# Softmax sums inverted once per batch element, and row maxima turned on TensorE and masked into extra query rows

## What is computed

```python
x = x + xattn(layernorm(x), ctx)    # 16 heads of 96, 4 key/value heads
x = x + ffn(layernorm(x))           # 8 experts of 512 x 512, the mean of the top 2
# xattn, per batch element:
hidden = concatenate([context, latents])            # 1556 rows
q = latents @ Wq.T; k = hidden @ Wk.T; v = hidden @ Wv.T
attn = softmax(q @ k / sqrt(96)); out = (attn @ v) @ Wo.T
# ffn: logits = x @ W_gate + b_gate; y = relu(x @ W_e + b_e), averaged over the two best experts
```

## Time and profile before

| | us |
|---|---|
| runs | 3805.85, 3798.13, 3792.36 (median 3798.13) |
| profiled execution | 3799.79 |
| its span | 3798.0 |
| TensorE busy | 3615.9 (95%) |
| VectorE busy | 2438.7 (64%) |
| ScalarE busy | 1740.3 (46%) |
| GpSimd busy | 829.2 (22%) |
| mean granted clock of TensorE | 0.979 |

### The profile page before, as it was taken

The page is one execution under the profiler, slowest core; times in us unless marked ns, Lnnn a source line. Parts: engine busy times, 40 slices in busy tenths (PEclk is TensorE's granted clock), DMA queues, the critical chain, the costliest instruction groups (busy, mean ns, idle before and its releaser), DMA issues. The chain is left out here.

```text
span 3798.0 us, 66233 instructions
## 1 busy us (share of the span) xinstructions
PE 3615.9 (95%) x22164; PEld 3291.2 (87%) x22164; DVE 2438.7 (64%) x3568; ACT 1740.3 (46%) x3236; POOL 829.2 (22%) x440
## 2 busy tenths in 40 slices
PE   8999999999999999999999999999999999888999
PEld 7888888888888888888888888888888889766887
DVE  4356666666666666666666666666666666645544
ACT  3234444554545544555545455445555545423222
POOL 0132222222222222222222222222222221431000
PEclk9999999999999999999999999999999999998999
DMA  6531111111111111111111111111111111474100
GB/s 217 199 98 47 47 47 47 47 47 47 47 47 47 47 47 47 47 47 47 46 42 47 47 47 47 47 47 47 47 47 47 47 47 37 120 213 140 39 33 31
DMA packets 302735, 240.04 MB, mean 63 GB/s; under 512 B 197346, under 2 KB 263138, under 8 KB 302066
## 3 DMA queue, kind: packets, MB, share of 16 engines
q1 hardware_dynamic: 302706, 239.69, 21.8%
HBM read 184.38 MB, written 55.22 MB: 63 GB/s over the span
## 5 line engine op out<-in xcount | busy, mean ns | idle before, releaser
L746 PE MATMUL ps_proj<-wv_hi,parts 128*125 128x384 f32 x3072 | 893.4, 347 | 0.0
L135 POOL TENSOR_SCALAR parts<-raw 128x1000 fp32r<-128x1000 f32 (+1 forms) x198 | 267.1, 1349 | 2480.8 <-PE ps_proj L746 2293.1
L680 DVE TENSOR_TENSOR probs_lo<-probs,probs_hi 125x448 fp32r<-125x448 f32 (+1 forms) x896 | 660.8, 754 | 100.2 <-ACT probs_hi L604 76.0
L733 PE MATMUL ps_proj<-parts,wk_hi 128*128 128x500 f32 x2304 | 710.9, 390 | 4.7 <-DVEq L636 4.7
L746 PEld LDWEIGHTS ps_proj<-wv_hi,parts 128*125 128x125 f32 x3072 | 582.3, 193 | 1.6
L650 DVE TENSOR_TENSOR values_lo<-ps_proj,values_hi 125x384 fp32r<-125x384 f32 x384 | 210.7, 555 | 571.9 <-ACT values_hi L588 570.9
L596 ACT ACTIVATE probs<-ps_scores 125x448 f32<-125x448 f32 (+1 forms) x896 | 462.0, 516 | 168.5 <-PE ps_scores L797 130.9
L746 PE MATMUL ps_proj<-wv_lo,parts 128*125 128x384 f32 x1536 | 531.1, 346 | 0.0
L733 PEld LDWEIGHTS ps_proj<-parts,wk_hi 128*128 128x128 f32 x2304 | 431.7, 188 | 94.3 <-DVEq L636 5.1
L137 POOL TENSOR_TENSOR parts<-raw,parts 128x1000 fp32r<-128x1000 f32 (+1 forms) x198 | 496.1, 2505 | 16.5
L604 ACT CAST probs_hi<-probs 125x448 fp32r<-125x448 f32 (+1 forms) x896 | 484.0, 540 | 28.5
(11 more groups left out here) (149 smaller groups left out, 5983.8 us busy)
## 6 DMA issues: line engine op xcount, KB each, us to landing
raw<-in_ctx SPq DMA_DIRECT2D x192, 500.0 KB, 3.6
qk_hi<-proj_out_hi SPq DMA_DIRECT2D x60, 224.0 KB, 2.0
qk_lo<-proj_out_lo SPq DMA_DIRECT2D x60, 224.0 KB, 2.2
queries_hi<-qk_hi SPq DMA_DIRECT2D x32, 336.0 KB, 3.6
queries_lo<-qk_lo SPq DMA_DIRECT2D x32, 336.0 KB, 3.6
att_t<-attended SPq DMA_DIRECT2D x128, 84.0 KB
raw<-att_t SPq DMA_DIRECT2D x7, 768.0 KB, 6.7
att<-att_t SPq DMA_DIRECT2D x7, 768.0 KB, 7.8
```

Of the source, the lines that this page charges most:

```text
L680: dve.tensor_tensor(prs[1][0:R, u % PRING, 0:N], pr[0:R, u % PRING, 0:N], f(prs[0][0:R, u % PRING, 0:N]), ALU.subtract).then_inc(p_lo, 1)
L733: mm = pe.matmul(pproj[n % 2][:, 0:CS], w["wk"][a][:, j // 3, i * P:(i + 1) * P], ct[v][:, c, j // 3, :], start=(j == 0), stop=(j == 3 * K ...
L746: mm = pe.matmul(pproj[n % 2][0:VT, 0:KD], ct[a][:, t // VTC, j // 3, s], w["wv"][v][:, j // 3, :], start=(j == 0), stop=(j == 3 * KT - 1))
```

## The change

Sums: `store` now copies and stores all 97 rows of a head, so the plain row sums go to a DRAM tensor. In the next batch element, SyncE loads the 16 x 56 sums of the one before, VectorE inverts them in one instruction behind unit 14, and SyncE stores the inverses to DRAM, where `combine` reads them as before. SyncE's store waits for VectorE. The sums of batch element 30 are handled between the loop and the loads of the output weights, those of 31 at the start of `combine`.

Maxima: `mrow` is transposed on TensorE (`turn_max`, behind value tile 5), and VectorE multiplies the first eight rows of the result, repeated eight times, with a mask that keeps each half of a group's queries in its own row (`place_max`). They become rows 96 to 103 of `queries_hi`; rows 96 to 103 of `keys_lo` are -1. The diagonals, the matmuls with ones and ScalarE's copy go. `READY = 6`: the first scores come one value tile later, behind tile 6. The parts are spread as one behind each of the six key tiles of chunks 1 and 2, and two in each of the value tiles 0 to 4.

```diff
...
-READY = 5
+READY = 6
...
+def load_sums(sp, stream, scratch, b):
+    sp.dma_start(stream["sums"][:], scratch["z"].rearrange("h (b q) -> b h q", q=Q)[b]).then_inc(stream["sums_loaded"], 16)
+def invert_sums(dve, stream, b):
+    dve.wait_ge(stream["sums_loaded"], b * 16 + 16)
+    dve.reciprocal(stream["inverse"][:], stream["sums"][:]).then_inc(stream["inverted"], 1)
+def store_inverse(sp, stream, scratch, b):
+    sp.wait_ge(stream["inverted"], b + 1)
+    sp.dma_start(scratch["rz"].rearrange("h (b q) -> b h q", q=Q)[b], stream["inverse"][:]).then_inc(stream["inverse_stored"], 16)
...
-def early_parts(c, i):
-    first = (c - 1) * KV
-    return [(0, 0), (first, first + 1), (first + 1, first + 3), (first + 3, first + 4)][i + 1 if c else 0]
+def key_part(c, i):
+    return (c - 1) * KTILES + i
+def value_parts(t):
+    first = (CHUNKS - 1) * KTILES + 2 * t
+    return first, first + 1
...
 def attend(nc, w, stream, io, scratch):
...
         with nc.Block() as block:
             @block.sync
...
-                def store_sums(b, h):
-                    sp.wait_ge(z_inverted, START + b * H + (h + 1) * G)
-                    sp.dma_start(rz_d[bass.ds(b, 1), h * G:(h + 1) * G, :],
-                                 osb[HD:HD + 1, h % 2, :].rearrange("d (h q) -> d h q", q=Q)).then_inc(stored[h % 2], 16)
                 def store(b, h):
...
-                    if h < KV - 1:
-                        store_sums(b, h)
+                    sp.dma_start(z_d[bass.ds(b, 1), h * G:(h + 1) * G, :],
+                                 osb[HD:HD + 1, h % 2, :].rearrange("d (h q) -> d h q", q=Q)).then_inc(stored[h % 2], 16)
...
-                sp.wait_ge(consts, 5)
+                sp.wait_ge(consts, 3)
                 load_v(0)
-                with sp.Fori(0, B - 1) as b:
+                def batch(b, first=False):
                     for n in range(LOADS):
...
+                    if not first:
+                        for i in range(2):
+                            sp.wait_ge(stored[i], START + b * 64)
+                        load_sums(sp, stream, scratch, b - 1)
+                        store_inverse(sp, stream, scratch, b - 1)
                     for h in range(KV - 1):
...
                     load_v(b + 1)
...
-                    store_sums(b, KV - 1)
+                batch(0, first=True)
+                with sp.Fori(1, B - 1) as b:
+                    batch(b)
+                for i in range(2):
+                    sp.wait_ge(stored[i], START + (B - 1) * 64)
+                load_sums(sp, stream, scratch, B - 2)
+                store_inverse(sp, stream, scratch, B - 2)
                 for n in range(LOADS):
...
                 for h in range(2):
...
                 for i in range(2):
...
+                sp.wait_ge(inverse_stored, (B - 1) * 16)
...
                 for h in range(2, KV):
...
-                store_sums(B - 1, KV - 1)
                 for i in range(2):
...
             @block.gpsimd
             def _(pool):
...
+                for n, ap in enumerate((f(vt_hi[:, NVT]), f(vt_lo[:, NVT]), mrow[:], ident[:], own[:])):
+                    pool.memset(ap, 0.0).then_inc(cleared, 1)
+                    pool.wait_ge(cleared, n + 1)
+                for n, (ap, value) in enumerate(((kt[1][HD:HD + HALVES], -1.0), (vt_hi[:, 0:NVT, :, HD:HD + 1], 1.0),
+                                                 (vt_hi[0:Q, NVT, :, HD:HD + 1], 1.0))):
+                    pool.memset(f(ap), value).then_inc(consts, 1)
...
+                pool.affine_select(out=ident[:], in_=ident[:], compare_op=ALU.not_equal, fill=1.0, base=0,
...
+                pool.wait_ge(consts, 4)
+                pool.affine_select(out=own[:], in_=own[:], compare_op=ALU.not_equal, fill=1.0, base=0,
+                                   pattern=[[-1, HALVES], [0, HALF]], channel_multiplier=1).then_inc(consts, 1)
...
-                    act.copy(osb[0:HD, h % 2, :], pav[0:HD, h % 2, 0:GQ]).then_inc(o_copied, 1)
+                    act.copy(osb[:, h % 2, :], pav[0:HD + 1, h % 2, 0:GQ]).then_inc(o_copied, 1)
...
                 with act.Fori(0, B) as b:
                     for c in range(CHUNKS):
...
                             keys(b, c, i)
                     for t in range(NVT):
                         values(b, t)
-                        if t == READY:
-                            act.wait_ge(mb_done, b + 1)
-                            act.copy(q[0][HD:HD + 1, :], pav[HD:HD + 1, :, 0:KV * HALF]).then_inc(mneg_done, 1)
                         if t >= READY:
...
             @block.vector
             def _(dve):
...
-                    dve.tensor_reduce(mrow[:].unsqueeze(2), mpart[:], AX.X, ALU.max).then_inc(mrow_done, 1)
-                    dve.wait_ge(mrow_done, b + 1)
-                    for i in range(2):
-                        shape = [HALF, KV, HALF]
-                        dve.tensor_tensor(mdiag[:, i, :].rearrange("p (a b) -> p a b", a=KV),
-                                          negident[:].unsqueeze(1).broadcast_to(shape),
-                                          mrow[:, i * KV:(i + 1) * KV].unsqueeze(2).broadcast_to(shape),
-                                          ALU.mult).then_inc(mdiag_done, 1)
+                    dve.tensor_reduce(mrow[:, 0:HALVES].unsqueeze(2), mpart[:], AX.X, ALU.max).then_inc(mrow_done, 1)
+                def place_max(b):
+                    dve.wait_ge(max_turned, b + 1)
+                    shape = [HALVES, HALVES, HALF]
+                    dve.tensor_tensor(q[0][HD:HD + HALVES, :].rearrange("p (a b) -> p a b", a=HALVES),
+                                      pav[0:HALVES, 0, 0:HALF].unsqueeze(1).broadcast_to(shape), own[:],
+                                      ALU.mult).then_inc(max_in_queries, 1)
...
-                def invert_sums(b, h, g):
-                    dve.wait_ge(pv_done, START + b * NU + (h + 1) * UNITS)
-                    dve.wait_ge(stored[h % 2], START + b * 64 + 32 * (h // 2))
-                    s = slice(g * Q, (g + 1) * Q)
-                    dve.reciprocal(osb[HD:HD + 1, h % 2, s], pav[HD:HD + 1, h % 2, s]).then_inc(z_inverted, 1)
                 def batch(b, first=False):
                     for c in range(CHUNKS):
                         for i in range(KTILES):
                             keys(b, c, i)
-                            n = c * KTILES + i
-                            if not first and n < G:
-                                invert_sums(b - 1, KV - 1, n)
-                            for p in range(*early_parts(c, i)):
-                                part_max(b, p)
+                            if c > 0:
+                                part_max(b, key_part(c, i))
                     for t in range(NVT):
-                        p = EARLY_PARTS + 2 * t
+                        p, last = value_parts(t)
                         if p < PARTS:
...
+                        if t == READY - 1:
+                            place_max(b)
                         values(b, t)
                         if p < PARTS:
-                            part_max(b, p + 1)
-                        if p + 2 == PARTS:
+                            part_max(b, last)
+                        if last + 1 == PARTS:
...
                         if t > READY:
...
                     for u in range(NVT - READY - 1, NU):
...
-                        if u > UNITS and 1 <= u % UNITS < 1 + G:
-                            invert_sums(b, u // UNITS - 1, u % UNITS - 1)
+                        if u == 2 * UNITS and not first:
+                            invert_sums(dve, stream, b - 1)
...
-                for g in range(G):
-                    invert_sums(B - 1, KV - 1, g)
...
             @block.tensor
             def _(pe):
...
-                def spread_max(b):
-                    pe.wait_ge(mdiag_done, 2 * b + 2)
+                def turn_max(b):
+                    pe.wait_ge(mrow_done, b + 1)
...
-                    pe.wait_ge(z_inverted, START + b * H)
-                    for i in range(2):
-                        mm = pe.matmul(pav[:, i, 0:KV * HALF], ones[:], mdiag[:, i, :], start=True, stop=True)
-                    mm.then_inc(mb_done, 1)
+                    pe.transpose(pav[:, 0, 0:HALF], mrow[:], ident[:]).then_inc(max_turned, 1)
...
                 def scores(b, u):
...
                         if u == 0 and n == 0:
...
-                            pe.wait_ge(mneg_done, b + 1)
+                            pe.wait_ge(max_in_queries, b + 1)
...
                     if j == 0 and h >= 2:
...
-                        pe.wait_ge(z_inverted, START + b * H + (h - 1) * G)
...
                     for n, t in enumerate(tiles):
...
                     for c in range(CHUNKS):
                         for i in range(KTILES):
...
-                            for p in range(*early_parts(c, i)):
-                                max_scores(b, p)
+                            if c > 0:
+                                max_scores(b, key_part(c, i))
```

(46 more changed lines are left out.)

7 lines of the change are left out of this document (4 added, 3 removed).

## The result

The changed kernel takes 3634.29 us (median of four runs, 3631.96 to 3637.84) against 3801.99 before; the ratio is 0.9562, with a 95% interval of 0.954 to 0.9585. The profiled execution took 3633.99 us, 165.8 less than that of before. The gain was forecast at 135 us, 31 too little.

The account below looks back on a forecast made before the run. The prediction took TensorE, busy 95% of the span, as the bound. Its terms, 91.3 - 8 + 43 + 10 + 18 - 18.6 - 0.6 = 135 us, off the profiled 3799.8 gave 3664.5 us, range 3638 to 3708.

Parts of the forecast that it names:

- the spread maxima: TensorE's waits for the maxima parts in key and value tiles: 10 us gained, bounds -5 and 25.
- the transpose: New 112-column transpose on TensorE behind value tile 5: 0.25 us each, 32 times, costing 8 us.
- the tile gap: TensorE between value tiles 5 and 6: waits and matmuls with ones go, 91.3 us gained.
- the tail: Last batch element: output-weight loads behind the inverses' store start GpSimd 18.6 us later, costing 18.6, bounds 14 and 23.
- the reciprocals' term: TensorE's second wait for the probabilities in each loop element goes, the first stays: 18 us gained, bounds 0 and 35.
- case from below: Both waits for the probabilities gone (17) and the maxima's last waits gone (15 less) would give 3635 us.
- The mask: VectorE's 8 x 896 mask from PSUM takes 1.1 us, hidden behind value tile 6 and two score matmuls.
- The clock: TensorE's clock in the 31 loop elements returns to full: 43 us gained, bounds 0 and 43.
- rival 1: TensorE's clock stays low in the loop behind smaller remaining waits: 3707 us, or 3686 for half; chance 0.13.
- 2 (the slow mask): VectorE's mask takes 3.6 us, TensorE waits 1.7 us an element and the clock falls: 3760 us; chance 0.05.
- 4 (the waits move): Waits at the transpose, in value tile 0 and for the probabilities stay or grow: together 3718 us; chance 0.06.
- Rival 3: SyncE issues head stores late behind unit 14's inverses, stopping ScalarE and TensorE: slower, 3867 us at 6.5 us late; chance 0.03.

Follow-up runs that it names:

- before_ready_6: The kernel before with `READY = 6` and nothing else, diagonals and ones kept behind value tile 5: 3720.7 us, ratio 0.9787.
- spread_undone: The changed kernel with the parts of the maxima placed where they were before: 3643.3 us, ratio 0.9596 to the kernel before.
- maxima_only: The changed kernel with the old sums (512 reciprocals on one partition, stored per head): 3630.8 us, ratio 0.9551 to the kernel before.
- sums_only: The kernel before with the new sums alone, diagonals and ones as they were: 3779.4 us, ratio 0.9955.
- tail_fixed: The changed kernel with the six output-weight loads moved ahead of the store of batch element 30's inverses: 3619.1 us, ratio 0.9536 to the kernel before.

## Why the prediction was right in its direction, and wrong in its size

What bounds the kernel, that the place behind value tile 5 cost waits, matmuls and clock, and that the tail would lose: all held. The size was too small. The step that failed most is the term of the spread maxima, 10 us forecast and 20 measured; the transpose, the tile gap and the tail were each 4 us off in the same direction, and the reciprocals' term rested on a wait that the reciprocals do not cause. The range was too narrow below by the prediction's own numbers: its case from below, 17 and 15 us more than the forecast, gives 3632.5 (it says 3635), and its edge was set at 3638, above it. By its own steps, with the forecast and what was measured:

- **The tile gap, 91.3 forecast.** I took the six score matmuls at 0.13 us, from four that stood behind a refill. At full pace they start 0.108 apart (1430.13 to 1430.78, six of them, 0.65), so 3.0 us an element went, not 2.9: 4 us more.
- **The transpose, 8 us.** 0.12 us of TensorE's time each instead of 0.25, and no wait came before it: 4 us more. Its duration is 259 ns as median of 32 (259 to 287), over half of it beside the matmuls around it, so the cost can't be read off a duration; the prediction's lower bound, 0.1 for its pace alone, was close. The Trainium skill (TensorE: Matmul & The Clock Gate, Part 4: PE-mode transpose) gives 390 ns for a transpose by itself; that too is a duration, and it doesn't price the place either.
- **The mask, at nothing.** Right, 1.08 us against 1.1, in all 32 elements. By the Trainium skill's rule on VectorE instructions with two SBUF inputs (GPSIMD Engine Reference, Specifications) this one, with a single SBUF input, is not slowed, and the rows agree: 1082 to 1084 ns in 31 elements beside a splitting GpSimd, 1084 in the last beside an idle one.
- **The clock, 43.** Right in size, and now shown: before_ready_6 returns all of it. My reason was half right. I had set it down to both waits of the place, and in rival 1 to the longest; but the longest alone, 1.36 us, leaves the clock up, and so does 0.95 us alone. It fell only where both stand together.
- **The spread, 10.** The waits for the maxima lost 0.64 us an element, 20 us. I counted the refill of the new wait twice (0.43 us lost, not 0.6) and added a small wait behind it that never came, so 0.43 us an element was left where I had 0.75, 10 us in all. That the wait in key tile 4 would go was right, but either part of the change removes it: it is gone with the reciprocals away and the parts as before (spread_undone), and with the parts spread beside the reciprocals (maxima_only).
- **The reciprocals, 18.** 13.7 beside the new maxima, 30 alone. The wait that I expected to go did, but not for my reason: where only the reciprocals are taken away both waits stay (0.15 and 0.43 us, sums_only), and where only the first scores come one tile later the second is gone, with all the reciprocals in place (before_ready_6). The one that I expected to stay grew from 0.17 to 0.39. That the sum came near 18 is in part luck. What the new sums do take away is two small waits of `weigh` and, without the new maxima, the wait in key tile 4, where four reciprocals stood ahead of the parts.
- **The tail, -18.6.** 17.7 us later to start, but 14.1 at the end, since GpSimd's splits ran 2.8 us faster, for the most part beside an idle VectorE. A delay and its cost aren't the same where the delay changes who else is running.
- **`combine`, -0.6.** Not to be seen in a stretch that varies by 10 us.

The loop's terms sum to 153 forecast and 172 measured; this is where most of the miss lies, several small ones with the same sign. The measured terms, 94 for the gap less 4 for the transposes, 43, 20 and 14, come to 167: where the other 5 us lie isn't shown. The waits for the probabilities, two before and one now, are the likely place. Rivals 1 (the clock stays low), 2 (the slow mask) and 4 (the waits move) didn't come; the turn's margin held in each element. Rival 3 didn't come in the loop, since SyncE had its 5 us to spare (in one element head 0's store is issued at 1460.51 and ScalarE copies head 2 at 1469.11, without waiting for a store), but its mechanism is what the last element shows: ScalarE 11.3 us at a store that stood behind the inverses.

What stays open: in which elements the clock falls. It is 24 of 31 before and 22 with the new sums alone, behind the same two waits; before, the two waits are 1.35 to 1.37 and 0.77 to 0.78 us in every one of the 31, so their sizes don't tell these elements from the others.

## What to carry to other kernels

A short stall of the bounding engine has a price beyond its length: look at the pace of the matmuls behind it before pricing its removal, and look first for one more tile of cover, which is three edited lines here and gave 77 us. When an instruction that waits for another engine is put into a DMA queue, list what stands behind it at the loop's end too: in the loop the stores behind it had time to spare, and behind the loop six loads that other work was waiting for came late and cost 14 us. And price parts of a change together as well as apart: the new sums were worth 30 us in the loop alone and 14 beside the new maxima.

## What the runs showed of the hardware

- TensorE's granted clock fell to 1.2 GHz behind two waits of 1.35 and 0.77 us that stood 0.9 us of matmuls apart, in 24 of 31 elements; behind 1.36 us alone (31 times) or 0.95 us alone (32 times) it never fell.
- A transpose of a 112 x 128 fp32 tile between other matmuls started 0.03 us before the next one and cost 0.12 us of TensorE's time in all, with a duration of 259 ns.
- A VectorE instruction of 8 x 896 elements with one PSUM and one SBUF input took 1082 to 1084 ns, with GpSimd splitting beside it (31 times) and idle (once). One of 112 x 448 with two SBUF inputs took 616 and 624 ns beside an idle GpSimd, in the last element, and 1430 to 2236 beside a splitting one. The other way round, GpSimd's two-input split of 128 x 1024 took 2.34 us beside a waiting VectorE, and 2.6 to 3.5 in tail_fixed, where VectorE was at work.
